# A transformer block on one core: attention's side jobs in two pieces, and three steps of scores in a row at corner quads

## What is computed

```python
x = x + 0.5 * ffn(layernorm(x))
x = x + attn(layernorm(x))
x = x + 0.5 * ffn(layernorm(x))

# ffn: xf [2048, 128]
logits = xf @ gate_w.T + gate_b
logits = logits * rsqrt(mean(logits * logits) + eps) * rms_w
g = max(softmax(logits / 0.5)); norm_g = g / (g + 1e-6)
h = gelu(einsum('nd,edh->neh', xf, w1) + b1)
out = ((einsum('neh,ehd->ned', h, w2) + b2) * norm_g).sum(experts)

# attn
xn = layernorm(x) * ln_w + ln_b
q, k, v = split(xn @ w_qkv)            # 8 heads of 8 columns each
q, k = l2norm(q), l2norm(k)
attn = softmax(where(causal, 8 * q @ k.T, min))
out = (attn @ v) @ w_out
```

## Time and profile before

| | |
|---|---|
| three runs, median | 269.8 us |
| profiled execution: its own time | 269.82 us |
| its span | 268.1 us |
| PE busy | 258.2 us (96%) |
| ACT busy | 217.5 us (81%) |
| DVE busy | 216.2 us (81%) |
| POOL busy | 80.7 us (30%) |
| granted clock of PE | 0.998 of full |

### The profile page before, as it was taken

The page is one execution under the profiler, slowest core; times in us unless marked ns, Lnnn a source line. Parts: engine busy times, 40 slices in busy tenths (PEclk is TensorE's granted clock), DMA queues, the critical chain, the costliest instruction groups (busy, mean ns, idle before and its releaser), DMA issues.

```text
span 268.1 us, 5428 instructions
## 1 busy us (share of the span) xinstructions
PE 258.2 (96%) x1829; PEld 183.6 (69%) x1829; DVE 216.2 (81%) x590; ACT 217.5 (81%) x344; POOL 80.7 (30%) x175
## 2 busy tenths in 40 slices
PE   7999999999999999979998999999999999999995
PEld 6886878888788786533434433378888887888783
DVE  7999899998898987797378587378889678697784
ACT  2897668859878889999999999987777867859673
POOL 6302104204850482664349545520200000200100
PEclk9999999999999999999999999999999999999999
DMA  5741200001012104101314003300004211210311
GB/s 152 219 123 23 58 1 2 0 1 39 2 34 46 42 2 78 40 1 22 62 39 82 2 4 78 80 1 4 0 8 111 42 39 39 39 34 9 80 39 39
DMA packets 33343, 11.51 MB, mean 43 GB/s; under 512 B 24130, under 2 KB 32548, under 8 KB 33316
## 3 DMA queue, kind: packets, MB, share of 16 engines
q1 hardware_dynamic: 33172, 11.11, 17.7%
q10 hardware_dynamic: 144, 0.07, 0.1%
HBM read 4.88 MB, written 2.62 MB: 28 GB/s over the span
## 4 chain that ended last, share of the span: by engine, by line
PE 73%; DVE 8%; ACT 7%; issue 5%; POOL 4%; DMA 2%; SPq 0%; POOLq 0%; DVEq 0%; ACTq 0%
PE ps L590 10%; PE ps L596 10%; PE ps L608 10%; PE ps L593 10%; PE ps L613 10%; PE ps L611 9%; PE ps L746 5%; ACT probs L937 3%; PE ps L708 2%; PE ps L777 2%; ACT h L924 2%; POOL probs L1533 1%; POOL w_raw L1527 1%; DMA kT<-k_stack 1%; DVE h_lo L1100 1%
## 5 line engine op out<-in xcount | busy, mean ns | idle before, releaser
L924 ACT ACTIVATE h<-ps,cols 128x512 f32<-128x512 f32 x128 | 88.0, 694 | 36.2 <-PE ps L596 32.6
L1100 DVE TENSOR_TENSOR h_lo<-h,h_hi 128x512 fp32r<-128x512 f32 x128 | 88.6, 698 | 19.1 <-ACT h_hi L927 16.7
L937 ACT ACTIVATE probs<-ps 128x1024 f32<-128x1024 f32 (+1 forms) x80 | 65.0, 918 | 1.5 <-PE ps L708 1.4
L590 PE MATMUL ps<-xT_hi,w_hi 128*128 128x512 f32 x128 | 51.5, 402 | 0.0
L608 PE MATMUL ps<-h_hi,w_hi 128*128 128x512 f32 x128 | 50.5, 395 | 0.3 <-ACT yT L949 0.3
L927 ACT ACTIVATE h_hi<-ps,cols 128x512 fp32r<-128x512 f32 x73 | 50.2, 688 | 0.0
L613 PE MATMUL ps<-h_lo,w_hi 128*128 128x512 f32 x128 | 50.2, 392 | 0.0
L596 PE MATMUL ps<-xT_lo,w_hi 128*128 128x512 f32 x128 | 49.9, 390 | 0.0
L593 PE MATMUL ps<-xT_hi,w_lo 128*128 128x512 f32 x128 | 49.9, 390 | 0.0
L611 PE MATMUL ps<-h_hi,w_lo 128*128 128x512 f32 x128 | 49.9, 389 | 0.0
L746 PE MATMUL ps<-probs,v_ones 128*32 128x512 f32 (+4 forms) x384 | 34.2, 458 | 0.9 <-POOL probs L1533 0.6
(11 more groups left out here) (141 smaller groups left out, 273.2 us busy)
## 6 DMA issues: line engine op xcount, KB each, us to landing
w_raw<-in_L_ffn_w SPq DMA_DIRECT2D x8, 256.0 KB, 4.6
turned<-blocks SPq DMA_DIRECT2D x6, 256.0 KB, 2.0
w_raw<-turned SPq DMA_DIRECT2D x24, 64.0 KB, 2.3
w_raw<-v_ones SPq DMA_DIRECT2D x8, 128.0 KB, 2.4
x_sb<-in_L_attn_x SPq DMA_DIRECT2D x3, 256.0 KB, 6.8
out_x<-x_sb SPq DMA_DIRECT2D x3, 256.0 KB, 2.3
w_raw<-o_scaled SPq DMA_DIRECT2D x2, 256.0 KB, 4.3
x_sb<-in_L_attn_x SPq DMA_DIRECT2D x2, 128.0 KB, 2.3
```

What stands on the lines that cost most here:

```text
L590: pe.matmul(bank, w1_hi[:, w], xT_hi[:, cols_g], start=True, stop=False)
L924: first = nc.scalar.activation(h[:, slot, :], ps[:, BANK_H + slot, :], ACT.Gelu, bias=bias)
L937: nc.scalar.activation(probs[:, s % P_SLOTS, :, 0:width], ps[:, bank:bank + 2, 0:width], ACT.Exp, scale=SCALE).then_inc(exp_done, 1)
L1100: dve.tensor_tensor(h_lo[:, slot, :], h[:, slot, :], h_hi[:, slot, :].bitcast(f32), ALU.subtract).then_inc(split_done, 1)
```

## The change

Jobs are cut into two pieces that stand behind different quads: the table now has a pair of quads for each job, fill has a second argument for the piece, and only the second piece tells DVE that the bank is full. The order of the jobs is new: ln, then both halves of qkv, then the projections; the layer norm of the second network moves from quad 23 to 27 and 28, its gate from 24 to 30. At the corner quads 12, 19, 22, 25 and 32 PE issues scores 2k, 2k + 1 and 2k + 2 in a row and outputs(k) behind them; scores 2k + 3 follow, then outputs(k + 1). Behind attention, the normalisation and turn of group F = 6 move on DVE from before the second network into it, behind chunk 1 of F = 4, and its features are taken at chunks 9 and 10 instead of 4 and 8.

```diff
-AT_FIRST = dict(AT, gate_product=6, gate_logits=6, gate_shift=11, gate_tanh=13, gate_weight=14, ln_copy=4, ln_low=8,
+AT_FIRST = dict(AT, gate_product=6, gate_logits=6, gate_shift=11, gate_tanh=13, gate_weight=14, ln_copy=9, ln_low=10,
...
-        jobs = [(q1, "ln", LAST), (q1 + 2, "project", (0, 0)), (q1 + 4, "project", (0, 1)),
-                (q1 + 5, "qkv", 0), (q1 + 7, "qkv", 1), (q2 + 3, "ffn_ln", 0),
...
+        jobs = [((q1, q1 + 1), "ln", LAST), ((q1 + 2, q1 + 4), "qkv", 0), ((q1 + 5, q1 + 6), "qkv", 1),
+                ((q1 + 7, q1 + 8), "project", (0, 0)), ((q1 + 9, q1 + 11), "project", (0, 1)),
...
-        gate_at = {q2 + 4: GROUPS, quad_steps - 3: GROUPS + 1}
+        gate_at = {q3 + 4: GROUPS, quad_steps - 3: GROUPS + 1}
...
-        TANH_AT = 62
+        TANH_AT = 72
...
+            def fill(n, piece):
+
+                quads, kind, arg = jobs[n]
                 bank = ps[:, job_bank(n), :]
...
+                if piece == 0:
+                    if n:
+                        pe.wait_ge(job_emptied, n)
...
+                elif kind == "qkv":
+                    i = halves[arg][piece]
+                    m = pe.matmul(bank[:, 192 * piece:192 * piece + 192], xf[:, ATT, P * i:P * i + P], wqkv_sb[:, :],
+                                  start=True, stop=True)
...
+                if piece:
+                    m.then_inc(job_filled, 1)
...
             for k in range(quad_steps):
                 short = steps[2 * k]["last"] and k < quad_steps - 1
                 if k == PV_LAG - 1:
                     third_products(0)
-                scores_of(2 * k)
-                if short:
+                three = short and k > last_quad[1]
+                ahead = k and steps[2 * k - 1]["last"] and k - 1 > last_quad[1]
+                if not ahead:
+                    scores_of(2 * k)
+                if short and not three:
                     outputs(k)
                 scores_of(2 * k + 1)
-                if not short:
+                if three:
+                    scores_of(2 * k + 2)
+                if not short or three:
                     outputs(k)
...
+                        if c == 1:
+                            normalise(FFN, GROUPS + 2, 2)
+                            turn_features(GROUPS + 2)
...
                 if (kind, arg) == ("qkv", 1):
                     own_squares(LAST)
                     square_sums(LAST)
                     guesses(LAST)
                     inverse_lengths(dve, LAST)
                     unit_vectors(dve, LAST)
+                if (kind, arg) == ("project", (0, 0)):
                     stacks(LAST)
...
-                if s == 2 * last_quad[2] + 1:
+                if s == 2 * last_quad[5] + 1:
                     ln_once(GROUPS)
-                if s == 2 * last_quad[5] + 1:
-                    gate_root(GROUPS)
                     ln_once(GROUPS + 1)
                 if s == 2 * last_quad[6] + 1:
-                    ln_once(GROUPS + 2)
+                    gate_root(GROUPS)
+            ln_once(GROUPS + 2)
```

More of the change, by code:

```diff
@@ L264, in build @@
         q1, q2, q3 = first_of_pair[1:]
-        jobs = [(q1, "ln", LAST), (q1 + 2, "project", (0, 0)), (q1 + 4, "project", (0, 1)),
-                (q1 + 5, "qkv", 0), (q1 + 7, "qkv", 1), (q2 + 3, "ffn_ln", 0),
[L267 to L270, removed]
+        jobs = [((q1, q1 + 1), "ln", LAST), ((q1 + 2, q1 + 4), "qkv", 0), ((q1 + 5, q1 + 6), "qkv", 1),
+                ((q1 + 7, q1 + 8), "project", (0, 0)), ((q1 + 9, q1 + 11), "project", (0, 1)),
+                ((q2 + 1, q2 + 3), "project", (1, 0)), ((q2 + 4, q2 + 5), "project", (1, 1)),
+                ((q3 + 1, q3 + 2), "ffn_ln", 0), ((q3 + 5, q3 + 6), "project", (2, 0)),
+                ((q3 + 8, q3 + 9), "project", (2, 1)), ((quad_steps, quad_steps), "project", (pairs - 1, None))]
         job_number = {(kind, arg): n for n, (_, kind, arg) in enumerate(jobs)}
-        gate_at = {q2 + 4: GROUPS, quad_steps - 3: GROUPS + 1}
+        pieces_at = {quad: (n, piece) for n, (quads, *_) in enumerate(jobs[:-1]) for piece, quad in enumerate(quads)}
+        gate_at = {q3 + 4: GROUPS, quad_steps - 3: GROUPS + 1}
         LATER_GATES = {0: GROUPS + 1, 2: GROUPS + 2, 3: GROUPS + 3}
-        TANH_AT = 62
+        TANH_AT = 72
         def gate_of(layer, g):
@@ L296, in job_bank @@
         def job_bank(n):
-            at = jobs[n][0]
+            at = jobs[n][0][0]
             return 13 - output_bank(steps[2 * min(at, quad_steps - 1)]["unit"] // QUADS)
         def pair_of_job(n):
-            return steps[2 * min(jobs[n][0], quad_steps - 1)]["unit"] // QUADS
+            return steps[2 * min(jobs[n][0][0], quad_steps - 1)]["unit"] // QUADS
         by_dma = [("features", F) for F in range(GROUPS + 1, 2 * GROUPS)] + [("y", F) for F in range(GROUPS, 2 * GROUPS - 1)]
@@ L646, in ffn_group @@
                     if layer == 1 and first and c == 3:
-                        fill(len(jobs) - 1)
+                        fill(len(jobs) - 1, 0)
+                        fill(len(jobs) - 1, 1)
                     if c == at["gate_product"] and gate_product_of(layer, g) is not None:
@@ L724, in pv @@
                 if opens and pair > 1:
-                    pe.wait_ge(job_emptied, sum(at < k for at, *_ in jobs))
+                    pe.wait_ge(job_emptied, sum(quads[1] < k for quads, *_ in jobs))
                     pe.wait_ge(gate_logits_done, GROUPS + sum(quad < k for quad in gate_at))
@@ L750, in pv @@
                 m.then_inc(pv_done, 1)
-            def fill(n):
-                at, kind, arg = jobs[n]
+            def fill(n, piece):
+                quads, kind, arg = jobs[n]
                 bank = ps[:, job_bank(n), :]
[L756 to L763, removed]
+                if piece == 0:
+                    if n:
+                        pe.wait_ge(job_emptied, n)
+                    gates = sum(quad < quads[0] for quad in gate_at)
+                    if gates:
+                        pe.wait_ge(gate_logits_done, GROUPS + gates)
+                    if n == 0 or pair_of_job(n) != pair_of_job(n - 1):
+                        pe.wait_ge(o_copied, pair_of_job(n))
                 if kind in ("ln", "ffn_ln"):
@@ L775, in fill @@
                     pe.wait_ge(o_ready, pair + 1)
-                    for tile in tiles if half is None else [tiles[i] for i in halves[half]]:
-                        m = pe.matmul(bank[:, tile], o_feat[:, tile], wout_sb[:, :], start=True, stop=True)
-                m.then_inc(job_filled, 1)
+                    for i in halves[piece] if half is None else halves[half][piece:piece + 1]:
+                        m = pe.matmul(bank[:, P * i:P * i + P], o_feat[:, P * i:P * i + P], wout_sb[:, :], start=True, stop=True)
+                if piece:
+                    m.then_inc(job_filled, 1)
             def keep_busy(times):
@@ L804, in _ @@
             pe.wait_ge(wout_in, 16 * HEADS)
-            next_job = 0
             def scores_of(s):
@@ L827, in outputs @@
                     pv(quad)
-                    if jobs[next_job][0] == quad:
-                        fill(next_job)
-                        next_job += 1
+                    if quad in pieces_at:
+                        fill(*pieces_at[quad])
                     if quad in gate_at:
-                        pe.wait_ge(job_emptied, next_job)
+                        pe.wait_ge(job_emptied, sum(quads[1] <= quad for quads, *_ in jobs))
                         gate_product(gate_at[quad], 13 - output_bank(steps[2 * quad]["unit"] // QUADS))
@@ L1387, in _ @@
             normalise(ATT, LAST, LAST)
-            for n, (at, kind, arg) in enumerate(jobs[:-1]):
+            for n, (_, kind, arg) in enumerate(jobs[:-1]):
                 if n == 0 or pair_of_job(n) != pair_of_job(n - 1):
@@ L1394, in _ @@
                     stacks(LAST - 1)
-                if (kind, arg) == ("project", (0, 1)):
-                    dve.wait_ge(job_emptied, n + 1)
-                    first_stats(GROUPS)
                 if (kind, arg) == ("qkv", 1):
```

27 lines of the change are left out of this document (12 added, 15 removed).

## The result

The changed kernel takes **274.59 us** (six runs, 274.54 to 274.84) against 269.78 (six runs): 1.018 times the time before, with an interval of 1.0167 to 1.0193. The forecast was 273.9, its range 271.8 to 275.2. The profiled execution takes 274.54 us with a span of 272.8 [before 268.1], so the 4.7 us lie inside the span.

What follows compares the result with a forecast made beforehand. ACT's exponentials bound attention, TensorE the second network. 269.8 + 3.1 (corners) + 1.3 (DVE wait) - 0.3 (pieces) + 0 (behind attention) = 273.9 us; own range 272.9 to 274.8 (68%), full range 271.8 to 275.2.

Steps and rivals of the forecast that it cites:

- corners: Attention, quads 12, 19, 22, 25, 32: output behind three scores delays the next exponential; 4.8 us late against 1.7, +3.1 us.
- job 4 waits for DVE: Behind quad 15: TensorE waits 1.9 us until DVE, after its Newton block, empties job 3; exponential 38 late, +1.3 us.
- behind jobs and pieces: Attention: half jobs nearly fit a wide quad's slack but pay their ends; 1.2 us of loss becomes 0.9, -0.3 us.
- behind attention: Group 2's normalisation and turn move into the second network; 2.7 us lead against 1.9, so 0, up to 1.0.
- the signs named 0.7 to 1.2: Exponentials 26, 40, 46, 52, 66 each start 0.7 to 1.2 us after ACT is free, when an output product ends.
- the removed wait is real, but the code puts another in its place: Corner quads: exponential 2k + 2 needs the output of quad k - 3, now behind scores waiting for exponential 2k - 1.
- 1.5 to 2 us: Sign: TensorE stands idle 1.5 to 2 us behind the output of quad 15 until DVE's addition to x_sb.
- fill idle time: Other moves of DVE and POOL (gate, statistics) cost nothing: DVE is busy 46.02, POOL 35.98 of 67.85 us in attention.
- the slot wait doesn't bind: Rival, faster (5%): at corners output k - 3 is through before ACT finishes the two small steps; 268.2 us.
- The second network: Rival (8%): 1.9 us of DVE work or late features reach TensorE in the second feed-forward network; 274.9 us.
- The clock: Rival (3%): TensorE's new 1.9 us wait in attention drops its clock to 1.2 GHz, two quads lose 1.7; 275.6 us.

Runs made afterwards that it cites:

- ten slots: Changed kernel with 10 instead of 8 slots for probs (probabilities): 274.69 us, five runs. The kernel before with 10 slots, as a control: 269.80 us.
- the last two kernels: Changed kernel with the old corner order, first addition before Newton steps, F = 5 features earlier: 269.44 us; the same with both corner scores before the output: 269.25 us.
- The first kernel of the experiments: Changed kernel with corner quads in the order of before (scores, output, scores), pieces and new job order kept: 271.55 us, ratio 1.0061.
- one with the same wait: Changed kernel with the cast and subtraction of group 5's features moved ahead of gate_weight on DVE: five runs, 273.78 to 275.45 us, ratio 1.0172.

## Why the prediction was right, step by step

| step | forecast, us | measured, us |
|---|---|---|
| corners | +3.1 | 5.3 - 1.7 = +3.6 in the trace; alone +4.3, taken out of the change -3.0 |
| job 4 waits for DVE | +1.3 | +1.02 in the trace; taken out alone -0.5 |
| behind jobs and pieces | -0.3 | 1.1 - 1.5 = -0.4 |
| behind attention | 0 | +0.7 |
| sum | +4.1 | +4.9 of terms; span +4.7, median +4.8 |

The forecast is 0.7 us below the median, inside its own range of 272.9 to 274.8. Part of that is cancellation: the corners and what lies behind attention were put 0.5 and 0.7 too low, and the wait for DVE and the pieces together 0.4 too high.

**Corners.** The mechanism is the predicted one: late exponentials 26, 40, 46, 52 and 66, the end of an output as releaser, 25 on its cadence. The starts are late by 0.82 to 1.38 us, where the signs named 0.7 to 1.2. Five late starts were put at 4.8 and are 5.3. In each some 0.1 us is the time from the output's end to the exponential, taken as 0.03 and read as 0.12 or 0.13 at all five corners. The scores ahead of the output start 0.14 us behind exponential 23's end at quad 12, not 0.06. Quad 32 is 1.35 where 1.1 stood. Against that, quad 19 is only 0.87 instead of 1.1, because exponential 38 is itself late there: without that wait it is 1.32. The words "the removed wait is real, but the code puts another in its place" held, but the place of the loss was not quite right. The working priced it at the slot, with TensorE's wait for exponential 2k - 1 as a link of the chain; the loss comes from that wait, and with ten slots it only moves to other exponentials.

**The wait for DVE.** Predicted as 1.9 us of TensorE's idle and 1.3 us at exponential 38, it is 1.41 and 1.02, so the sign "1.5 to 2 us" was just missed. DVE's block took 138.70 - 132.73 = 5.97 us to the start of the addition, not 6.38, which is nearly all of the difference: the Newton steps run 0.15 faster, and from the unit vectors to the next instruction it is 0.61 instead of 0.84. What the working did not see is that this term and the corners share: removed by itself it gives 0.5.

**Pieces.** The size is about as forecast: -0.4, or -0.2 without the two exponentials behind a tanh (from 1.2 to 1.0). A piece of two takes 0.41 us (139.18 to 139.59), put at 0.44. That the gain is no larger was laid to the corners, and the last two kernels bear that out in part: without the corner stalls the late starts behind jobs are 0.9 instead of 1.1.

**Behind attention.** Here a step failed, if only by 0.7 us: the term put at nothing. The prediction looked for the cost of the moved DVE work in the second network, and that held: 88.00 of 88.00. It took the other moves as "fill idle time", by DVE's busy share. But the reading of F = 5 stands on DVE behind the list of jobs. The list has as many jobs as before, but its last addition moved from quad 30 to quads 34 and 35, from 162.57 to 173.40 us. So the reading slid by 8.2 us, half of which is attention as a whole being late: it started 4.1 us ahead of exponential 79 before, and starts with it now. That took it from a stretch where POOL is idle onto POOL's last masks. The first kernel of the experiments shows that this goes with the jobs' new order and not with the corners; moving it back gives 0.75 in the runs with a full clock. The rows show that DVE's two instructions are no longer than before (0.39 and 0.69, before 0.43 and 0.69) and POOL's two masks 0.76 longer. The first, at 176.01, takes 0.58 us beside the cast, and the second, at 176.54, 0.77 beside the subtraction, 0.29 being the usual. The same is seen once more in this trace, at 138.22, where a mask takes 0.72 us beside the unit vectors (138.09, 0.69). The Trainium skill, "SBUF — State Buffer", "Who interferes with whom", has VectorE and GpSimd sharing a pair of ports, on which an instruction of VectorE with two SBUF inputs, and some casts, shut GpSimd out until they end. By its rule the later one stands still for the whole instruction. The rows roughly agree for the second mask, which starts 0.07 behind the subtraction. They don't for the first: it had started 0.03 before the cast and still paid, and the two masks lost 0.76 us where cast and subtraction last 1.08 together. That it is the ports and not another thing beside them wasn't tried separately.

**The rivals.** That three in a row would be faster since "the slot wait doesn't bind" fell twice: the slot does bind, and without it nothing is won. The second network paid nothing. The clock did not fall in the changed kernel, but by its mean did in three of five runs of one with the same wait, and in two of five of another, at a price of 1.4 to 1.8 us where 1.7 stood; 3% was low. Nothing in these runs tells why the six kept their clock, so that part of the hit may be luck.

## What to carry to other kernels

Putting more scores ahead of an output helps only if these can be issued: here the third stood behind an exponential that was not done, and the engine idled with ready work queued behind it. More slots for what stands behind don't mend that. The wait itself comes from the three sets of PSUM banks for scores; a fourth set was not tried. A late start at one place and one a few quads on are not a sum, so a fix is measured together with what stands behind it. When a list of side jobs ends later, look where everything behind the list on that engine slides to, and what the other engines do there.

## What was not expected of the hardware

- POOL's masks of 128x128: two in 0.54 us with DVE idle or busy on small things, 1.30 and 1.31 us in three kernels beside DVE's cast and subtraction of 128x512 from SBUF to SBUF, whose own lengths don't grow.
- TensorE's granted clock fell to 0.50 within 2 us after a single wait of 1.41 us, in one profiled execution of each of two kernels. By the mean clock (0.994 or less) it fell in three of five and two of five of their runs, which then take 1.4 to 1.8 us longer; in the six of the changed kernel and the five of the one with its jobs alone, which have the same wait, it did not. The kernels without that wait never show a mean under 0.997. What decides is open.
- An exponential starts 0.12 or 0.13 us behind the recorded end of the output that it waits for, at all five corners.
